# Feed-forward of one expert moved ahead of an attention, and the router with it

## The chip, the cores and the metric

One core of a Trainium2 chip runs the whole program in one launch. TensorE does the matrix products and transposes into PSUM, VectorE (DVE in the profile) and ScalarE (ACT) read PSUM and write SBUF, GpSimd (POOL) works in SBUF and issues some transfers, SyncE (SP) issues the others. Each engine runs its own instructions in order and waits on semaphores. The metric is the device time of one launch in microseconds.

## The reference

Four sequences (B = 4) of 512 tokens with 288 channels go through four transformer layers, with one conditioning vector for each sequence. All is float32. Each layer is

```
mod = silu(c) @ w_ada + b_ada                    # six rows of 288 per sequence
h   = ln(x) * (1 + scale_msa) + shift_msa
q, k, v = split(h @ w_qkv + b_qkv)               # 16 heads of 18
x  += gate_msa * (softmax(q k^T / sqrt(18)) v @ w_proj + b_proj)
h   = ln(x) * (1 + scale_mlp) + shift_mlp
x  += gate_mlp * ffn(h)
```

In layers 1 to 3 `ffn` is gelu(h W1 + b1) W2 + b2 with 1152 hidden channels. In layer 0 it is a mixture of four such experts: `h @ w_gate` gives four logits, the two highest get the softmax of the two as weights and the others zero, and the output is the weighted sum of all four experts, which are all computed for all tokens. The attention of layer 2 is written like the others.

## The kernel before

`plan` is a Python function that writes one list of steps, and `build` walks this list once for each engine: what a step does on an engine is queued there in the order of the list. So the order of `put` calls is the order on every engine, and the planner's work is to interleave generators. It keeps a planned TensorE time `pe[0]`, the sum of `PE_NS` over the steps put.

The index i = 4 * layer + sequence runs from 0 to 16. An iteration has two parts.

- Attention of i: `at_steps(i)` puts 16 `s2` steps (scores again, transposed, and exp on ScalarE, L1316) and `av` steps (L1721), and beside them `pre(i+1)`: the rows of the next sequence turned (`turnx`, L1644) and its q and k (`proj_qk`). `proj_v(i+1)` follows.
- Feed-forward of i - 1: `ffn_steps(i-1)` puts `fc1` steps (two weight tiles of 128 hidden channels by 256 tokens, 14 matmuls, L1817; gelu on ScalarE, L1353 and L1354; the low half `hid` on VectorE, L1590) and, two double tiles later, the `fc2` steps (L1832, with the bias at L1830). An expert has 18 tiles: two halves of the tokens by nine tiles. After each half `residual` scales two results by the gates (L1535, VectorE) and adds them to X (L1225, GpSimd). The loop `weave` runs these steps as the main line and lets others advance beside them whenever the planned time has gone on by their gap: `mid(i)` (output projection of i, residual, norm, turn of the rows for the feed-forward, in layer 0 the router; gap `MID_NS`, 3500 in the iterations 1 to 4) and `side`, the score stream of i + 1 (gap `S1_NS`, 5000).

The score stream `s1_steps` puts pairs of score matmuls (L1698), whose row maxima VectorE takes from PSUM (MX at L1470), and after every eight pairs a `rows` step (L1704, a turn of the maxima, with a transfer into QS). A sequence has 32 pairs. `at_steps` advances the stream one step at each `s2` and forces what a group of heads still lacks. The router `route(i)` is 28 narrow matmuls (`rt`, L1801), then small VectorE steps `rtk`, `rte`, an exp on ScalarE and `rtw`, which writes the gates CW.

Matrix products are done with weights split in two parts. A weight chunk is transferred into one of two buffers ST, cast by ScalarE (FH, L1346), its rest subtracted by GpSimd (FL, L1220) and its tail mended by VectorE (`fix`, L1365). Nine chunks make an expert; `prep_f` does one, and may write a place of FH only when the fc2 of the expert before has read it (`w_free`). The list `jobs` fixes the order in which weights are transferred, two jobs ahead; those of the feed-forward, three chunks in a job of seven transfers, are issued by SP, others by GpSimd. Background steps sit in `bg`; `finish_bg(1000)` at the end of an iteration puts all that is left.

In iteration 0 there is no feed-forward to run. The order is attention of sequence 0, `proj_v(1)`, and then `mid(0)` with the score stream of sequence 1 and the background advancing one step each at every step of `mid(0)`. Its end is the router of sequence 0. Iteration 1 is the attention of sequence 1, and then all four experts of sequence 0.

## Time and profile before

| | us |
|---|---|
| median of 3 runs | 2354.89 (2349.18 to 2356.09) |
| profiled execution | 2348.38 |
| its span | 2346.7 |
| TensorE busy | 2084.9 (89%) |
| VectorE busy | 1292.9 (55%) |
| ScalarE busy | 1159.1 (49%) |
| GpSimd busy | 485.3 (21%) |

Busy times are sums over the instructions of an engine within the span; matmuls are pipelined, so that a busy TensorE is not one at its peak. The granted clock of TensorE is given as a share of full speed, 2.4 GHz; 0.50 is its low level of 1.2 GHz. PE is TensorE, PEld its weight loads. Times within the span count from its start. In the profiled execution the attention of sequence 1 begins near 223 us, the feed-forward of sequence 0 near 275, and the attention of sequence 2 near 461.

### The profile page before, as it was taken

Reading aid. Unit: us, or ns where it says so; the run is one execution under the profiler, and the core shown is the slowest. Engines: PE = TensorE matmul, PEld = TensorE weight load, DVE = VectorE, ACT = ScalarE, POOL = GpSimd, SP = SyncE. Lnnn points to the kernel's source line nnn. Section 1 sums busy time; section 2 is a strip of 40 time slices with the busy share of each in tenths; the row PEclk is TensorE's granted clock in tenths of the full one; section 3 lists DMA queues with packets and bytes.
Section 4 is the critical chain, followed back from the end, with each engine's and each line's share of the span. In section 5 each row is a group of like instructions: output and inputs, shape, how many; then the busy total and the mean of one; then the engine's idle time right before and its main releaser. Section 6 shows DMA issues by size and latency. Waiting matters only on the chain.

```text
span 2346.7 us, 39460 instructions
## 1 busy us (share of the span) xinstructions
PE 2084.9 (89%) x15784; PEld 1536.6 (65%) x15784; DVE 1292.9 (55%) x2749; ACT 1159.1 (49%) x1797; POOL 485.3 (21%) x502
## 2 busy tenths in 40 slices
PE   6978999879989998999899999978988988899988
PEld 4443588738874886588466556877877637374748
DVE  3747355645664667465638482443424847674733
ACT  2353525554546365545635555534435273737363
POOL 3020033414440343044310100022210101100001
PEclk9685999989989998999998999997898989999999
DMA  4242422333234123423231412344253241323111
GB/s 147 61 132 47 115 67 69 78 90 97 68 97 112 52 86 64 119 68 89 72 98 14 125 7 62 42 92 103 44 109 58 72 90 37 83 44 88 31 14 24
DMA packets 204732, 173.99 MB, mean 74 GB/s; under 512 B 54822, under 2 KB 164678, under 8 KB 204550
## 3 DMA queue, kind: packets, MB, share of 16 engines
q1 hardware_dynamic: 197974, 158.76, 28.9%
q0 software_dynamic: 6576, 12.71, 1.9%
q8 instruction: 125, 2.05, 0.4%
q14 instruction: 57, 0.47, 0.1%
HBM read 125.57 MB, written 40.11 MB: 71 GB/s over the span
## 4 chain that ended last, share of the span: by engine, by line
PE 54%; DVE 21%; ACT 12%; issue 6%; POOL 3%; DMA 3%; SPq 2%; ACTq 0%; POOLq 0%; DVEq 0%
PE PSA L1817 13%; PE PSA L1832 9%; DVE MX L1470 8%; PE PSA L1721 6%; ACT PB L1316 4%; PE PSA L1668 4%; PE PSA L1611 4%; PE PSA L1711 4%; PE PSA L1698 4%; POOL FL L1220 2%; DVE HH L1590 2%; PE PSA L1634 2%; PE PSA L1741 1%; PE PSA L1680 1%; DVE FH L1365 1%
## 5 line engine op out<-in xcount | busy, mean ns | idle before, releaser
L1470 DVE TENSOR_REDUCE MX<-PSA 128x1 f32<-128x512 f32 x768 | 488.9, 683 | 317.5 <-PE PSA L1698 315.0
L1817 PE MATMUL PSA<-A,FH 128*128 128x256 f32 x2520 | 444.3, 291 | 26.1 <-DVE HH L1590 19.0
L1832 PE MATMUL PSA<-FH,HH 128*128 128x288 f32 x2016 | 449.5, 314 | 13.1 <-DVE HH L1590 13.0
L1353 ACT ACTIVATE HH<-PSA 128x512 fp32r<-128x512 f32 x252 | 150.3, 596 | 616.4 <-PE PSA L1817 609.2
L1316 ACT ACTIVATE PB<-PSA 128x1024 f32<-128x1024 f32 x384 | 370.7, 1027 | 103.3 <-PE PSA L1711 102.8
L1817 PEld LDWEIGHTS PSA<-A,FH 128*128 128x128 f32 x2520 | 363.8, 194 | 50.0 <-issue 20.1
L1832 PEld LDWEIGHTS PSA<-FH,HH 128*128 128x128 f32 x2016 | 331.0, 196 | 54.5 <-issue 36.6
L1832 PE MATMUL PSA<-FL,HH 128*128 128x288 f32 x1008 | 303.8, 301 | 0.0
L1220 POOL TENSOR_TENSOR FL<-ST,FH 128x544 fp32r<-128x544 f32 x171 | 240.2, 1418 | 233.9 <-ACT FH L1346 233.5
L1225 POOL TENSOR_TENSOR X<-X,TM 128x288 f32<-128x288 f32 x176 | 140.2, 811 | 681.0 <-DVE TM L1535 680.9
L1698 PE MATMUL PSA<-KS,QS 54*128 54x512 f32 x768 | 236.1, 528 | 41.4 <-DVE MX L1470 28.4
L1590 DVE TENSOR_TENSOR HH<-PSA,HH 128x512 fp32r<-128x512 f32 x252 | 172.7, 685 | 111.7 <-ACT PSA L1354 109.4
L1721 PE MATMUL PSA<-PB,VT 128*32 128x512 f32 x1536 | 227.7, 659 | 0.0
L1817 PE MATMUL PSA<-A,FL 128*128 128x256 f32 x1008 | 209.9, 290 | 14.8 <-POOL FL L1220 10.3
L1711 PE MATMUL PSA<-QS,KS 56*128 56x512 f32 x768 | 176.3, 508 | 50.7 <-ACT PB L1316 31.8
L1832 PEld LDWEIGHTS PSA<-FL,HH 128*128 128x128 f32 x1008 | 196.9, 195 | 0.0
L1711 PEld LDWEIGHTS PSA<-QS,KS 56*128 56x128 f32 x768 | 71.6, 202 | 168.7 <-ACT PB L1316 85.9
L1698 PEld LDWEIGHTS PSA<-KS,QS 54*128 54x128 f32 x768 | 98.6, 208 | 122.6 <-DVE MX L1470 65.0
L1817 PEld LDWEIGHTS PSA<-A,FL 128*128 128x128 f32 x1008 | 158.4, 194 | 23.1 <-POOL FL L1220 22.1
L1354 ACT ACTIVATE PSA<-PSA 128x512 f32<-128x512 f32 x252 | 149.3, 593 | 0.0
L1233 POOL COPY OT<-OT 128x256 f32<-128x256 f32 x16 | 6.5, 404 | 637.3 <-DVE OT L1489 507.0
L1346 ACT CAST FH<-ST 128x672 fp32r<-128x672 f32 x171 | 123.2, 748 | 29.1 <-DMA ST<-in_L_cond_w 13.9
(160 smaller groups left out, 2502.9 us busy)
## 6 DMA issues: line engine op xcount, KB each, us to landing
qkd<-HH SPq DMA_DIRECT2D x48, 504.0 KB
ST<-in_L_cond_w SPq DMA_DIRECT2D x51, 432.0 KB
ST<-in_L_cond_w SPq DMA_DIRECT2D x102, 192.0 KB
QS<-qkd SPq DMA_DIRECT2D x88, 144.0 KB
KS<-qkd SPq DMA_DIRECT2D x88, 144.0 KB
QS<-qkd SPq DMA_DIRECT2D x144, 72.0 KB
KS<-qkd SPq DMA_DIRECT2D x144, 72.0 KB
ST<-in_L_cond_w SPq DMA_DIRECT2D x153, 48.0 KB
```

The costliest lines, as they stand in the source:

```text
L1220: e.tensor_tensor(r(lo), ST[k % 2][:, s0:s0 + nl], hi[:, 0:nl], ALU.subtract).then_inc(s_wlo, 1)
L1225: e.tensor_tensor(X[:, b * QT + q, :], X[:, b * QT + q, :], TM[m % 2][:, :], ALU.add).then_inc(s_res, 1)
L1316: e.activation(pbf[st % 3][:, p * 1024:(p + 1) * 1024], PSA[:, bk * 512:(bk + 2) * 512], ACT.Exp, scale=SCALE).then_inc(free[bk], 1)
L1353: e.activation(r(HH[u][:, 0, :]), PS[bk][:, :], gelu)
L1354: e.activation(PS[bk][:, :], PS[bk][:, :], gelu).then_inc(s_gelu, 1)
L1470: e.reduce_max(MX[p // 2 % 2][:, col:col + 1], PS[bk][:, :], axis=AX.X).then_inc(free[bk], 1)
L1590: e.tensor_tensor(r(HH[u][:, 1, :]), PS[bk][:, :], HH[u][:, 0, :], ALU.subtract).then_inc(free[bk], 1)
L1698: e.matmul(PS[bk][:, :], r(QS[64 * x:64 * x + 54, p, q * 128:(q + 1) * 128]), r(KS[64 * x:64 * x + 54, p, :]), start=True, stop=True).then ...
L1711: m = e.matmul(PS[bk + x][:, :], r(KS[64 * x:64 * x + 56, 2 * g + p, kt * 128:(kt + 1) * 128]), r(QS[64 * x:64 * x + 56, 2 * g + p, :]), s ...
L1721: m = e.matmul(PS[bk][32 * hh:32 * hh + 32, :], VT[:, kt, h * V1:h * V1 + 32], PB[st % 3][:, hh, :], start=(kt == 0), stop=(kt == 3))
L1817: m = e.matmul(PS[bk][:, s_ * 256:(s_ + 1) * 256], r(w_), r(x_[:, half * 256:(half + 1) * 256]), start=(z == 0), stop=(z == 6))
L1832: m = e.matmul(PS[bk][:, 0:C], r(HH[u][:, c, tk]), r(w_), start=False, stop=(j == NCH - 1 and z == 2))
```

## The change

- In iteration 0 `mid(0)` runs with the score stream of sequence 1 and the background only until the rows for the feed-forward are turned (`rows_turned`). Since the test is made after a step has been taken, the router's matmuls `rt` are put as well.
- Then come `gates(0, 1)`, which was put in the attention of sequence 1, the switch to the PSUM banks `RING_B`, and `ffn_steps(0, (0,))`: expert 0 of sequence 0, with one step of `mid(0)` beside each of its steps and a step of the score stream per 2500 ns.
- `route(0)` stands before `stats_ahead(2)` in `mid(0)` and not behind it.
- Iteration 1 runs `ffn_steps(0, (1, 2, 3))`, with the score stream of sequence 2 at a gap of 4000 and not 5000.
- The weight job order brings the three jobs of expert 1 before the modulation weights of layer 1.

```diff
--- before.py
+++ after.py
@@ -28,6 +28,7 @@
 PE_NS = {"fc1": 1650, "fc2": 400, "proj": 930, "v": 930, "v2": 930, "qk": 1650, "turnx": 500, "turno": 500,
          "s1": 230, "s2": 450, "av": 230, "no": 500, "rows": 350, "qk2": 1650, "s1b": 1700, "s2b": 3000, "av2": 2500, "no2": 500, "rt": 3100}
 MID_NS = (3500, 800, 600)
+S1_0_NS = (0, 2500, 4000)
 S1_NS = (5000, 400, 3000)
 MID_AT = (8000, 14000)
 QK_LAND = 12000
@@ -135,12 +136,15 @@
     k_ = 3
     for i_ in range(NI + 1):
         L_, b_ = i_ // 4, i_ % 4
+        if i_ == 0:
+            jobs += [("f", k) for k in range(3, 6)]
+            k_ = 6
         if L_ < 3 and b_ == 1:
             jobs += [("ada", L_ + 1, j) for j in range(3)]
         if L_ < 3 and b_ == 2:
             jobs += [("q", L_ + 1), ("v", L_ + 1)]
         if 1 <= i_ <= 4 or (i_ and b_ == 0):
-            n_ = min(3 * NE if i_ <= 4 else 3, 4 * NE * 3 + 9 - k_)
+            n_ = min(9 if i_ == 1 else 3 * NE if i_ <= 4 else 3, 4 * NE * 3 + 9 - k_)
             jobs += [("f", k) for k in range(k_, k_ + n_)]
             k_ += n_
         if L_ < 3 and b_ == 3:
@@ -621,7 +625,7 @@
     back = background()
     n_fc, n_f1, n_f2 = [0], [0], [0]
 
-    def ffn_steps(i):
+    def ffn_steps(i, experts=None):
 
         L = i // 4
         a_n = (i + 1) % 2
@@ -629,7 +633,7 @@
         n_first = NCH * (i * NE if L == 0 else 16 + (L - 1))
         base = n_fc[0]
         tiles = [(e_, half, j, n_first + NCH * e_ + j)
-                 for e_ in range(NE if L == 0 else 1) for half in range(2) for j in range(NCH)]
+                 for e_ in experts or range(NE if L == 0 else 1) for half in range(2) for j in range(NCH)]
         nu = len(tiles) // 2
         acc, hid = [None] * 2, {}
 
@@ -704,7 +708,7 @@
                     next(side, None)
                     last[n] = pe[0] + gap
 
-    last_fc1, turned_early = [-1], set()
+    last_fc1, turned_early, rows_turned = [-1], set(), set()
 
     def pre(i):
         if i not in turned_early:
@@ -723,14 +727,16 @@
         for _ in range(W_MID):
             yield
         yield from turn_x(norm_of[i], (i + 1) % 2, L, 2, b)
+        rows_turned.add(i)
         if i + 2 < NI:
             if i == 0:
+                yield from route(0)
                 yield from stats_ahead(2)
             while i + 2 not in stats_of:
                 finish_bg(1)
             normed(i + 2, 0, stats_of[i + 2])
             yield
-        if L == 0:
+        if L == 0 and i:
             yield
             yield
             yield from route(i)
@@ -781,7 +787,7 @@
             for n, turned in enumerate(at2_steps(i) if L == 2 else at_steps(i)):
                 if L == 2 or n >= TURN_AT and not turned:
                     next(nxt, None)
-                if n == 3 and i:
+                if n == 3 and i > 1:
                     gates(i - 1, 1)
                 step_bg(2 if i == 0 else 1)
                 if i == 0 and not gb_ready[0] and (0, 0) in gr_ready:
@@ -816,9 +822,13 @@
             bg += [split(("q", L + 1), "q"), split(("v", L + 1), "v")]
         kind = 0 if i - 1 < 4 else 2 if (i + 1) // 4 == 2 else 1
         if i == 0:
-            weave(m, ((side, 0, 0), (back, 0, 0)))
+            weave(itertools.takewhile(lambda _: not rows_turned, m), ((side, S1_0_NS[0], 0), (back, 0, 0)))
+            gates(0, 1)
+            ring_of[0] = RING_B
+            weave(ffn_steps(0, (0,)), ((m, 0, 0), (side, S1_0_NS[1], 0)))
         if i:
-            weave(ffn_steps(i - 1), ((m, MID_NS[kind], MID_AT[i == 11] if L == 2 else 0), (side, S1_NS[kind], 0)))
+            weave(ffn_steps(i - 1, (1, 2, 3) if i == 1 else None), ((m, MID_NS[kind], MID_AT[i == 11] if L == 2 else 0),
+                                       (side, S1_0_NS[2] if i == 1 else S1_NS[kind], 0)))
         weave(m, ((side, S1_NS[kind], 0),))
         finish_bg(1000)
         if b == 3 and L < 3:
```

## Rows read from the trace of the kernel before

**Rows 1.** The page, part 1: busy us (share of the span) xinstructions.

```profile
PE 2084.9 (89%) x15784; PEld 1536.6 (65%) x15784; DVE 1292.9 (55%) x2749; ACT 1159.1 (49%) x1797; POOL 485.3 (21%) x502
```

**Rows 2.** Busy us (count) by engine in a stretch, clock, DMA share, GB/s.

```profile
192.50:223.00 30.50, 21.36 (x58) 12.43 (x57) 25.64 (x75) 3.72 (x9) 0.00 (x0) 0.50 0.01 4
...
223.00:275.00 52.00, 49.58 (x292) 21.85 (x292) 18.09 (x50) 38.12 (x47) 0.40 (x1) 0.93 0.44 95
...
345.00:383.00 38.00, 33.66 (x243) 30.63 (x242) 24.01 (x52) 19.38 (x35) 16.07 (x15) 1.00 0.28 79
...
461.00:478.00 17.00, 7.54 (x32) 2.73 (x34) 6.30 (x17) 7.77 (x9) 9.39 (x13) 0.63 0.42 71
...
1355.00:1385.00 30.00, 28.35 (x170) 21.20 (x169) 27.67 (x63) 15.06 (x30) 1.56 (x2) 1.00 0.15 8
```

**Rows 3.** Waits, 192 to 223: who waited for whom, us, times, longest.

```profile
PEld PSA L1698 <- DVE MX L1470: 11.9, 19, 1.7
...
PE PSA L1704 <- DVE MX L1470: 4.7, 2, 4.3
```

**Rows 4.** The chain of waits, 303 to 313: start, us, what.

```profile
303.69 1.67 PE PSA L1817 x14
...
311.53 1.59 PE PSA L1832 x12
```

**Rows 5.** Groups by line, 275 to 470: busy us, mean ns, idle before.

```profile
L1830 PE MATMUL PSA<-B,ON 128*128 128x288 f32 x16 | 5.4, 334 | 0.0
...
L1698 PE MATMUL PSA<-KS,QS 54*128 54x512 f32 x44 | 11.5, 518 | 0.0
...
L1590 DVE TENSOR_TENSOR HH<-PSA,HH 128x512 fp32r<-128x512 f32 x36 | 24.7, 687 | 13.2 <-ACT PSA L1354 12.7
...
L1535 DVE SCALAR_TENSOR_TENSOR TM<-PSA,CW,GB 128x288 f32<-128x288 f32 x16 | 7.5, 509 | 1.2 <-PE PSA L1832 1.2
...
L1365 DVE TENSOR_TENSOR FH<-ST,FH 33x128 fp32r<-33x128 f32 x36 | 17.5, 487 | 12.7 <-ACT FH L1346 11.9
...
L1377 DVE TENSOR_TENSOR B<-B2S,B 2x288 fp32r<-2x288 f32 x4 | 6.1, 1528 | 0.1
```

**Rows 6.** Instructions in order of time, 186 to 232: start, us.

```profile
187.72 0.29 DVE L1365 TENSOR_TENSOR FH<-ST,FH 33x128 fp32r<-33x128 f32 x1
...
191.76 0.68 DVE L1449 TENSOR_TENSOR A<-HF,A 32x512 fp32r<-32x512 f32 x1
...
205.87 0.99 PE L1801 MATMUL PSA<-WG,A 128*128 128x4 f32 x4
...
211.63 0.35 PE L1801 MATMUL PSA<-WG,A 96*128 96x4 f32 x1
...
222.96 1.69 PE L1711 MATMUL PSA<-QS,KS 56*128 56x512 f32 x4
...
223.80 3.91 ACT L1316 ACTIVATE PB<-PSA 128x1024 f32<-128x1024 f32 x4 [2.15 <-PE PSA L1711]
...
231.28 0.73 PE L1711 MATMUL PSA<-QS,KS 56*128 56x512 f32 x4
```

**Rows 7.** Line L1470 alone, 192.5 to 223: durations, first and last.

```profile
L1470 DVE TENSOR_REDUCE MX<-PSA x30: 657/682/692, 193.1 to 221.9; 128x1 f32<-128x512 f32 x30
```

**Rows 8.** Line L1365 alone, 275 to 470: ns min/median/max.

```profile
L1365 DVE TENSOR_TENSOR FH<-ST,FH x36: 282/290/1345, 330.8 to 464.7; 33x128 fp32r<-33x128 f32 x36
```

**Rows 9.** Order of time after the last fc2 of sequence 0.

```profile
462.58 2.06 ACT L1346 CAST FH<-ST 128x672 fp32r<-128x672 f32 x3 [4.23 <-DMA ST<-in_L_cond_w]
...
464.55 3.90 ACT L1316 ACTIVATE PB<-PSA 128x1024 f32<-128x1024 f32 x4
...
477.17 0.79 PE L1698 MATMUL PSA<-KS,QS 54*128 54x512 f32 x1 [5.98 <-DVE MX L1470]
```

**Rows 10.** Last residuals of experts 0 and 3, sequence 0.

```profile
344.49 0.93 DVE L1535 SCALAR_TENSOR_TENSOR TM<-PSA,CW,GB 128x288 f32<-128x288 f32 x2
...
460.30 0.94 DVE L1535 SCALAR_TENSOR_TENSOR TM<-PSA,CW,GB 128x288 f32<-128x288 f32 x2 [0.16 <-PE PSA L1832]
```

## The prediction

> **What bounds the kernel now.** I read the page first, then the busy time by stretch, then the waits and the instruction order inside the stretch that the change rewrites. TensorE is busy 89% of the span [rows 1], so in most places a microsecond is won only by removing TensorE work or TensorE idleness. The change removes no work; it can win only where TensorE idles or runs at its low clock. In time order the part concerned is:
>
> - 155 to 223: `mid(0)` with the scores of sequence 1. From 192.5 to 223 VectorE is busy 25.6 of 30.5 us, while the granted clock is 0.50, the 1.2 GHz level [rows 2]. The waits name the row maxima, MX at L1470, as what the score matmuls waited for, 11.9 us over 19 waits, and the last turn of the maxima waited 4.3 us for one [rows 3]. VectorE sets the pace here; TensorE has room.
> - 223 to 275: attention of sequence 1, TensorE 49.6 of 52 us.
> - 275 to 461: the four experts of sequence 0 beside `mid(1)`. In a plain expert (345 to 383) TensorE is busy 33.7 of 38 us at clock 1.00, VectorE 24.0: TensorE sets the pace [rows 2].
> - 461 to 478: a start of attention in which TensorE does 7.5 us in 17 [rows 2].
>
> So the change moves one expert from a TensorE-paced stretch into a VectorE-paced one.
>
> **What one expert weighs.** Nine double tiles of 14 fc1 matmuls, 1.67 us, and 12 fc2 matmuls, 1.59 us [rows 4], are 29.3 us; four bias matmuls at 0.334 add 1.3 [rows 5]: 30.6 us of TensorE. On VectorE it brings nine `hid` at 0.687 (6.2), four residuals at 0.509 (2.0), nine `fix` at 0.487 for the next expert's weights (4.4) and the bias split, its longest part 1.5 and in all about 3 by my estimate from that row: 15.6 us [rows 5]. ScalarE's GELUs and casts and GpSimd's subtractions have room: ScalarE has 3.7 us and GpSimd none in the 30.5 us [rows 2].
>
> **The first stretch.** Up to the turn of the rows the order is as before; the last piece of it is the DVE op at 191.76, and the last weight chunk of expert 0 has its tail fixed at 187.72 [rows 6], so nothing of expert 0 is late. From 192.5 on I build the new stretch:
>
> - The router comes first. It took from 205.87 to 211.98, 6.1 us at the low clock [rows 6]. Nothing denser stands around it now than before: 6.1. VectorE has nothing to do meanwhile.
> - The expert, 30.6.
> - Scores. 30 maxima are left after 192.5 [rows 7], 15 pairs. The side is allowed one step per 2500 ns of planned time over 9 x (1650 + 4 x 400) = 29250 ns; with steps of 1650 and 800 that comes out as nine, of which eight are pairs and one is the turn of the maxima. The 44 matmuls of L1698 between 275 and 470 are busy 11.5 us, 0.26 each [rows 5]: eight pairs are 4.2, and with the turn some 4.4.
> - The expert starts at the low clock. At 223 dense work began at that level too: four matmuls at L1711 took 1.69 us at 222.96 and 0.73 at 231.28 [rows 6], 8 us later. I take some 6 us of work done at half pace: 3 more.
> - Stalls. A plain expert leaves 38.0 - 33.7 = 4.3 us of idleness [rows 2], for its chain of GELU, hid and fc2; here, with more on VectorE, 5.
>
> Sum 6.1 + 30.6 + 4.4 + 3 + 5 = 49.1 us in the place of 30.5: **+18.6**. Bounds: below, without ramp and with half the stalls, 43.6 (+13). Above, VectorE decides. Its work from 192.5 is 16 maxima (10.9), route and statistics about 9, the expert's 15.6, the rest 1.5: 37 us; at the density of the old stretch, 25.6 of 30.5 or 84%, it takes 44, and with the 6 us of the router in which it has nothing, 50. So the two engines come out level, and the bound above comes from the fixes, next.
>
> **The fixes.** The `fix` at L1365 takes 290 ns in the median and up to 1345 [rows 8], in a stretch where GpSimd writes FL right beside it. GpSimd has such work after 192.5 only in the new kernel. If each of nine fixes took 1.345, they would be 12.1 us and not 4.4, all ahead of maxima in VectorE's queue; VectorE's 37 become 45, the stretch 45 / 0.84 + 6 = 59 us, +29. I keep the mean row, since 36 fixes at 0.487 already hold the long ones; +29 is the end above. The Trainium skill, "SBUF — State Buffer", section "Who interferes with whom", says that a VectorE instruction with two SBUF inputs is locked out while a GpSimd instruction reads SBUF; these operations are such a pair, and the long fixes here agree with it.
>
> **The boundary to the attention of sequence 1.** The expert leaves three casts of the next expert's weights in front of the first exps. At the same kind of boundary, after 460.5, ScalarE waited 4.23 us for a weight transfer, cast until 464.6, and the first exp began at 464.55 [rows 9], 4.0 us after the last fc2; before, at 223, it came about 1 us after. +3. Queued behind are exps, so the score-probability matmuls wait. On SP three loads of seven weight issues now stand ahead of the transfers of the turned maxima; these are needed only in the attention. Seven score pairs have slid into this attention, 3.5 us of TensorE, which is busy 95% there: +3. It now starts at the full clock: the slow beginning between 223 and 231 is spared, -3. Bounds 0 to +8, value **+3**.
>
> **The stretch of three experts.** It loses 30.6 us of TensorE and one of four sets of chain and weight-change stalls. A plain period is (460.30 - 344.49) / 3 = 38.6 us [rows 10], of which about 2 us of scores and 2.5 us of `mid(1)` stay: -34. What could also be late: the plan hands one piece of `mid(1)` per 3500 ns; four experts fit about 31 of its 34 pieces, three only some 24. The whole router of sequence 1 then comes after the last fc2. It runs about 3 us on TensorE, work that exists in either kernel, and its small VectorE chain, some 4 us, holds up ScalarE's exp and the exps behind it. But there TensorE stood until 477.17 for maxima anyway [rows 9], so of 5 us I count 1. Value **-33**, bounds -36 to -28.
>
> **Sum.** 18.6 + 3 - 33 = -11.4 us. The profiled execution took 2348.4 us around a span of 2346.7; the median of three is 2354.9, 6.5 above it. Taken off the median: 2343.5. Since the three runs spread over 7 us, I say 2344.
>
> **Rivals.**
> 1. *VectorE decides the first stretch* (chance 0.20). For it: 84% busy before and nine more hid. Against it: a later stretch, 1355 to 1385, with one expert, scores and the other sequence's `mid`, runs VectorE at 27.7 and TensorE at 28.4 of 30 us at clock 1.00 [rows 2]. With stalls of 12 for 5: net -4, 2351; no measurable change.
> 2. *Every fix is a long one* (0.08), by GpSimd's reads beside it. Against it: the mean row. Net 29 + 3 - 33 = -1: 2354. The lock is the one that the page named with the fixes states.
> 3. *The weights land late, slower* (0.12). The third load of expert 1 can be issued only when the first load's last chunk is split, and this waits for fc2 tiles in the second half of expert 0. If it lands more than 13 us after the last fc2 (2 of casts behind it, against 1 us before: 14 in place of 3, and the gain is gone), ScalarE's in-order queue holds every exp of the attention; at 461 a jam of this kind cost TensorE 9.5 of 17 us [rows 2]. For it: that jam, and more issues on SP. Against: there the GpSimd queue and a waiting residual were part of it, and SP is free. A landing at 21 us costs 22 in place of 3: net +8, 2362.
> 4. *The clock stays low* (0.07). If waits for maxima keep TensorE at 1.2 GHz, as between 192.5 and 223, expert 0 costs 30 us more in place of 3: net +16, 2371. Against: clock 1.00 with VectorE busier still at 1355 [rows 2]. The Trainium skill ("TensorE: Matmul & The Clock Gate", "What's actually happening") says the low level is the default and activity releases it; the trace agrees in both stretches.
> 5. *It does not do what it says* (0.03): expert 0 waits for its weights or the gate row. 187.72 speaks against it. 2355.
>
> **Numbers.** Forecast 0.50; no change means within 0.3%, 7 us, about what a measurement can tell. The forecast case itself is faster by that in some 8 of 10, rival 1 in 3 of 10: faster 0.48. Same 0.32, slower 0.20, from rivals 3, 4 and part of 1 and 2. Range 2332 (both low bounds, -22) to 2362; the likeliest case's own is 2334 to 2354.
>
> **What would show it.** Right: nine fc1 groups between about 198 and 235 with granted clock 1.00 from about 206; the first exp of the attention at 240 to 246 instead of 223.8; seven pairs of maxima in the first half of that attention; only two weight changes in the next FFN stretch, which ends 8 to 14 us earlier than 460.5; `rt` of sequence 1 right after its last fc2. Wrong: clock 0.5 past 215 (rival 4), `fix` near 1.3 us on the mean (2), ScalarE waiting over 10 us on a weight transfer near 245 (3), or an attention after 460 whose exps start more than 5 us later relative to the last fc2 and push 477.17 along with them.

## The result, and the profile after

| | before | after |
|---|---|---|
| median (lowest to highest), us | 2352.41 (2349.18 to 2356.09, 4 runs) | 2327.69 (2324.43 to 2334.02, 4 runs) |
| ratio to before, 95% interval | | 0.9904 (0.9874 to 0.9934) |
| span of the profiled execution, us | 2346.7 | 2332.3 |

The kernel became 1% faster, twice what was forecast, and its time lies below the range. The page, part 1, and then the busy time by stretch (TensorE, its weight loads, VectorE, ScalarE, GpSimd, then granted clock, DMA share, GB/s) of the kernel after; they answer to [rows 1] and [rows 2]. The stretches are the router, expert 0 with scores, the attention of sequence 1, the three experts, and 17 us after the last fc2 of sequence 0.

```profile
PE 2071.9 (89%) x15784; PEld 1533.1 (66%) x15784; DVE 1297.3 (56%) x2749; ACT 1164.2 (50%) x1801; POOL 484.8 (21%) x502
```

```profile
197.50:203.60 6.10, 6.04 (x29) 6.04 (x29) 0.00 (x1) 0.00 (x0) 0.00 (x0) 0.50 0.70 88
203.60:248.60 45.00, 38.97 (x256) 34.93 (x257) 34.05 (x82) 21.35 (x37) 12.39 (x13) 0.91 0.19 28
248.60:302.10 53.50, 47.52 (x280) 19.68 (x280) 32.50 (x67) 40.33 (x48) 7.00 (x8) 0.90 0.30 102
305.90:448.40 142.50, 133.84 (x941) 119.64 (x940) 76.87 (x151) 59.15 (x104) 47.73 (x44) 0.94 0.26 75
448.40:465.40 17.00, 9.71 (x52) 5.84 (x51) 10.87 (x38) 7.71 (x11) 8.38 (x12) 0.65 0.48 86
```

The expert stretch of before by the same view, for the comparison that decides:

```profile
274.80:460.60 185.80, 173.46 (x1208) 155.90 (x1206) 101.42 (x196) 77.18 (x134) 64.14 (x58) 0.93 0.26 74
```

The profiles do not locate the whole gain. From the end of the turn of the rows to the end of the span it is 2154.3 us before and 2134.8 after, 19.5 less, and 2151.1 and 2133.5, 17.6 less, in a second pair of profiles (again_before, again_after), where the medians differ by 24.7 and 29.2. The ledger below accounts for the 17 to 20; where the rest sits no profile shows.

**One table of marks for all runs.** What lies before the turn of the rows differs by 9 us between executions whose order there is the same (the turn ends between 188.6 and 197.5), so I count from that turn. Its end is the end of the VectorE step that stands at 191.76 in [rows 6]: 192.4. Marks: A, first L1711 of the attention of sequence 1 (L1721 after); V2, next values product; F, first fc1 of the experts in iteration 1; R, end of their last fc2; V3, the values product after it; V6, the values product at the end of iteration 4. All in us, from one profile each; V2 to F is 3.7 to 3.8 everywhere.

| kernel | turn-A | A-V2 | F-R | R-V3 | turn-V3 | V3-V6 | timed ratio |
|---|---|---|---|---|---|---|---|
| before | 30.5 | 48.1 | 185.8 | 67.4 | 335.5 | 663.2 | 1 |
| after | 51.1 | 53.4 | 142.5 | 62.4 | 313.3 | 668.2 | 0.9904 |
| again_before | 30.5 | 48.2 | 185.7 | 67.5 | 335.7 | 662.6 | one run |
| again_after | 51.1 | 53.7 | 139.9 | 64.1 | 312.6 | 665.9 | 0.9878 |
| late_route | 30.5 | 47.8 | 179.2 | 70.6 | 332.0 | 666.4 | 0.9963 |
| before_gap_4000 | 30.5 | 48.2 | 188.5 | 56.3 | 327.4 | 671.3 | 0.9986 |
| before_both | 30.5 | 48.1 | 183.4 | 58.2 | 324.0 | 667.3 | 0.9967 |
| early_route | 51.1 | 54.1 | 157.9 | 59.9 | 326.7 | 668.8 | 0.996 |
| gap_5000 | 51.1 | 53.7 | 140.2 | 86.8 | 335.6 | 666.1 | one run |
| gap_3000 | 51.1 | 54.2 | 153.0 | 59.4 | 321.5 | 670.3 | 0.9959 |
| q_sp_gap_5000 | 51.1 | 53.8 | 140.1 | 77.9 | 326.7 | 666.0 | 0.997 |
| scores_dense | 54.0 | 57.2 | 144.1 | 65.5 | 324.6 | 667.6 | one run |
| b2_first | 47.7 | 53.5 | 147.9 | 65.1 | 318.0 | 671.4 | 0.9934 |
| rt_later | 45.8 | 52.8 | 141.3 | 62.4 | 306.1 | 667.6 | 0.9883 |
| rt_b2 | 47.2 | 53.6 | 142.5 | 68.1 | 315.2 | 660.3 | 0.9857 |
| rt_b2_q_sp | 47.2 | 54.0 | 138.5 | 62.9 | 306.4 | 657.4 | 0.984 |
| combined | 47.3 | 54.1 | 138.5 | 67.9 | 311.5 | 653.4 | 0.984 |
| all_four | 47.2 | 53.7 | 142.6 | 64.4 | 311.8 | 652.4 | 0.9812 |

The first two columns repeat within 0.8 us between kernels with the same order there. F-R does not always: 142.5 and 139.9 in two executions of the changed kernel. A difference under 4 us there is no finding. The two profiles say what differed:

```profile
302.90:442.80 139.90, 131.20 (x942) 116.60 (x940) 76.85 (x151) 59.15 (x104) 47.71 (x44) 0.96 0.28 77
```

That is again_after, against the fourth line above: the same matmuls and, to 0.1, the same 8.7 us of idleness, with 2.6 us less of TensorE busy at a granted clock of 0.96 and not 0.94. So when F-R or R-V3 of two kernels are compared, busy time, idle time and clock have to be taken apart; I do so where a reading rests on it.

After against before: +20.6, +5.3, -43.3, -5.0 up to V3, in sum -22.2 by the marks, and +5.0 given back up to V6 (+3.3 in the second pair).

**The first stretch.** Order of time around 200 us on TensorE, after (start us, duration us, what; the idle time before it in brackets):

```profile
197.56 1.02 PE L1811 MATMUL PSA<-WG,A 128*128 128x4 f32 x4 [3.41 <-DVE A L1459]
...
203.56 1.20 PE L1827 MATMUL PSA<-A,FH 128*128 128x256 f32 x4
...
209.35 0.28 PE L1827 MATMUL PSA<-A,FH 98*128 98x256 f32 x1
...
241.57 0.54 PE L1842 MATMUL PSA<-FH,HH 128*128 128x288 f32 x2 [4.02 <-DVE HH L1600]
```

The router takes its 6.1 us; from 203.56 on work is dense, and its groups of four fc1 matmuls go from 1.20 to 0.71 us (granted clock 0.50 from 203 to 206, 0.69 to 209, 1.00 to 212). One long wait is left, 4.02 us for a `hid`. Here is what VectorE did in it, and beside it GpSimd:

```profile
233.74 1.35 DVE L1384 CAST B<-B2S 2x288 fp32r<-2x288 f32 x1
235.12 1.65 DVE L1387 TENSOR_TENSOR B<-B2S,B 2x288 fp32r<-2x288 f32 x1
236.81 1.35 DVE L1390 CAST B<-B2S 1x288 fp32r<-1x288 f32 x1
238.09 1.27 DVE L1480 TENSOR_REDUCE MX<-PSA 128x1 f32<-128x512 f32 x2
239.38 1.41 DVE L1375 TENSOR_TENSOR FH<-ST,FH 33x128 fp32r<-33x128 f32 x1
240.82 0.69 DVE L1600 TENSOR_TENSOR HH<-PSA,HH 128x512 fp32r<-128x512 f32 x1
```

```profile
235.11 5.53 POOL L1230 TENSOR_TENSOR FL<-ST,FH 128x544 fp32r<-128x544 f32 x4 [0.19 <-ACT FH L1356]
```

The bias split, 4.35 us in three operations, stands ahead of the `hid`, and so do the two maxima and a `fix` of 1.41 us. Line L1384 by itself shows that it need not be so long: four times, 298 ns at least, 299 in the median, 1349 at most.

```profile
L1384 DVE CAST B<-B2S x4: 298/299/1349, 233.7 to 439.2; 2x288 fp32r<-2x288 f32 x4
```

The two maxima, which read PSUM, keep their 0.64 us each beside the same GpSimd work.

**The attention of sequence 1** starts as said, with a late exp. ScalarE in order of time; it answers to [rows 9]:

```profile
248.44 2.06 ACT L1356 CAST FH<-ST 128x672 fp32r<-128x672 f32 x3 [4.62 <-DMA ST<-in_L_cond_w]
250.52 1.28 ACT L1326 ACT_TABLE_LOAD   x1
251.81 3.91 ACT L1326 ACTIVATE PB<-PSA 128x1024 f32<-128x1024 f32 x4
```

Of the delay, 1.28 us is a load of ScalarE's function table (ACT_TABLE_LOAD), since GELUs now stand ahead of these exps; the kernel has 35 such loads and had 31. The attention also starts at the low clock level again: its four matmuls of L1721 at 252.89 take 1.71 us, like those of L1711 at 222.96 in [rows 6].

### The profile page after: what moved, and what is told of

Read it like the earlier page. It is cut to its first block, busy times and chain, and to the rows that moved or that the text cites. A ratio compares the mean times of both kernels' runs of the same rounds, so it can differ in the third digit from the quotient of the medians.

```text
span 2332.3 us, 39462 instructions
## 1 busy us (share of the span) xinstructions
PE 2071.9 (89%) x15784; PEld 1533.1 (66%) x15784; DVE 1297.3 (56%) x2749; ACT 1164.2 (50%) x1801; POOL 484.8 (21%) x502
## 4 chain that ended last, share of the span: by engine, by line
PE 54%; DVE 20%; ACT 12%; issue 5%; DMA 4%; POOL 3%; SPq 2%; ACTq 0%; POOLq 0%; DVEq 0%
PE PSA L1827 13%; PE PSA L1842 10%; DVE MX L1480 8%; PE PSA L1731 5%; PE PSA L1621 4%; ACT PB L1326 4%; PE PSA L1721 4%; PE PSA L1678 4%; PE PSA L1708 3%; POOL FL L1230 2%; PE PSA L1644 2%; DVE HH L1600 2%; DVE FH L1375 2%; PE PSA L1751 1%; PE PSA L1690 1%
## 5 line engine op out<-in xcount | busy, mean ns | idle before, releaser
L1480 DVE TENSOR_REDUCE MX<-PSA 128x1 f32<-128x512 f32 x768 | 489.1, 682 | 324.0 <-PE PSA L1708 321.6
L1708 PE MATMUL PSA<-KS,QS 54*128 54x512 f32 x768 | 225.3, 516 | 31.9 <-DVE MX L1480 20.0
L1827 PE MATMUL PSA<-A,FL 128*128 128x256 f32 x1008 | 210.5, 291 | 15.5 <-POOL FL L1230 9.6
L1721 PE MATMUL PSA<-QS,KS 56*128 56x512 f32 x768 | 174.4, 505 | 55.3 <-ACT PB L1326 36.1
L1721 PEld LDWEIGHTS PSA<-QS,KS 56*128 56x128 f32 x768 | 70.8, 201 | 172.0 <-ACT PB L1326 90.2
L1708 PEld LDWEIGHTS PSA<-KS,QS 54*128 54x128 f32 x768 | 93.8, 204 | 106.3 <-DVE MX L1480 47.7
L1375 DVE TENSOR_TENSOR FH<-ST,FH 33x128 fp32r<-33x128 f32 x171 | 104.9, 623 | 53.9 <-ACT FH L1356 49.6
```

Of the source, the lines that this page charges most:

```text
L1375: e.tensor_tensor(r(hi[64:R2 - 1, f0:f0 + nf]), ST[k % 2][64:R2 - 1, s0 + f0:s0 + f0 + nf], hi[64:R2 - 1, f0:f0 + nf], ALU.subtract).then_ ...
L1480: e.reduce_max(MX[p // 2 % 2][:, col:col + 1], PS[bk][:, :], axis=AX.X).then_inc(free[bk], 1)
L1708: e.matmul(PS[bk][:, :], r(QS[64 * x:64 * x + 54, p, q * 128:(q + 1) * 128]), r(KS[64 * x:64 * x + 54, p, :]), start=True, stop=True).then ...
L1721: m = e.matmul(PS[bk + x][:, :], r(KS[64 * x:64 * x + 56, 2 * g + p, kt * 128:(kt + 1) * 128]), r(QS[64 * x:64 * x + 56, 2 * g + p, :]), s ...
L1827: m = e.matmul(PS[bk][:, s_ * 256:(s_ + 1) * 256], r(w_), r(x_[:, half * 256:(half + 1) * 256]), start=(z == 0), stop=(z == 6))
```

## The experiments

In the line numbers of the changed kernel ten are added to those of before, in its variants up to 21; in variants of the kernel before three or fewer.

**1 and 2. Both kernels again.** No edit.

> The kernel before once more, for a second trace. Theory: turn to end of the attention of sequence 2 again 335 us within 2; the last fc2 of sequence 0 to the end of that attention 67 us; the turn anywhere from 190 to 198. Rival: the jam after the last fc2 is a matter of this one execution; then 67 becomes 55 and the stretch is some 12 us shorter.

> The changed kernel once more, for a second trace and a tighter ratio. Theory: the whole gain lies between the turn of sequence 0's rows and the end of the attention of sequence 2 (before 192.4 to 528.0, 335.5 us; after 313.3), and what the first trace shows ahead of it (+5.1 us) is not of the change. Expected: that stretch again 311 to 315 us, the start of it anywhere from 190 to 198, the time 22 us below before (ratio 0.990 to 0.992). Rival, that the +5 ahead is caused by the changed order of the weight transfers: the turn again at 197 to 198.

Before 2348.13 us in one run, after 2325.74, ratio 0.9878 (0.9859 to 0.9897). The marks repeat: the gain and its places are not an accident of one execution. The turn of the changed kernel's rows ends at 194.3 here and not at 197.5, so that the late turn of the first profile is not of the change.

**3. late_route.** The kernel before, with the router of sequence 1 after the last fc2, where the changed kernel has it.

```diff
+            while i == 1 and ffn_done[0] < 0:
+                yield
             yield from route(i)
```

> The kernel before, and in iteration 1 the router of sequence 1 waits until the last fc2 of sequence 0 is put. It tests where the 9 us come from by which the stretch of three experts fell short of my sum. Theory A (the router's place): beside the experts the router costs TensorE 3 to 4 us and its chain more, while after them it is hidden by GpSimd's jam (weight issues for layer 1, then the waiting residual); then this alone gives -4 to -9 us: first fc1 to last fc2 from 185.8 to 177 to 182, last fc2 to the end of the attention 67.4 within 2. Rival B: nothing to gain there, the router's chain is added after the experts as fast as it leaves them: 0 within 3 us in all.

2345.97 us, 0.9963 (0.9938 to 0.9987). The experts take 6.6 us less, the stretch after them 3.2 more. Where the 6.6 sit is to be read in the chain of waits of the kernel before, 411 to 450:

```profile
415.95 1.59 PE PSA L1832 x12
...
428.16 3.02 PE PSA L1801 x28
431.18 0.58 PE PSA L1698
431.76 3.14 PE PSA L1832 x12
434.90 1.67 PE PSA L1817 x14
```

The 28 narrow matmuls cost 3.02 us, and the twelve fc2 matmuls behind them 3.14 in place of 1.59. In the stretch of before from 421 to 440 the granted clock was 0.91, from 345 to 421 it was 1.00; in the changed kernel it is 1.00 from 345 to 448. So the router costs TensorE its own 3.0 us and, after it, 1.5 us at the low clock level. Much of the rest stands near the end of the last expert, the kernel before first, then late_route:

```profile
455.05 0.73 PE L1832 MATMUL PSA<-FH,HH 128*128 128x288 f32 x2 [2.30 <-DVE HH L1590]
```

```profile
447.37 0.54 PE L1835 MATMUL PSA<-FH,HH 128*128 128x288 f32 x2 [0.96 <-DVE HH L1593]
```

In the kernel before two operations of the router's gates (L1554 and L1557, 1.36 us from 452.99 on) stand ahead of that `hid` on VectorE; TensorE waits 1.3 us longer and then works from 455 to 459 at a granted clock of 0.57, where late_route has 1.00 from 430 to the last fc2. Over the whole of F-R TensorE is busy 6.0 us less in late_route and idle 0.5 less: 3.0 are the router's own matmuls, the other 3.0 the same matmuls at a higher granted clock.

**4. early_route.** The changed kernel with the gap of `mid(1)` at 2300 and not 3500, so that the router comes while the three experts run.

```diff
-            weave(ffn_steps(i - 1, ...), ((m, MID_NS[kind], ...
+            weave(ffn_steps(i - 1, ...), ((m, 2300 if i == 1 else MID_NS[kind], ...
```

> The changed kernel, with mid(1) in iteration 1 at a gap of 2300 and not 3500, so that its router runs beside the three experts as before. Theory A: the router comes back onto the experts' stretch, first fc1 to last fc2 from 142.5 to 147 to 151, the rest unchanged or a jam of 5 to 7 us more in the attention: +4 to +9 us in all. Rival B: 0 within 3.

2343.27 us, 0.996 (0.9937 to 0.9983): more than half of the gain is gone. F-R is 15 to 18 longer, more than the theory's 4 to 9, R-V3 2.5 to 4 shorter. Of the 15 to 18, 4.3 are idleness of TensorE (13.0 for 8.7) and 11 to 14 are busy time (144.9 us for 133.8 and 131.2; the router's own matmuls are some 3 of it, the granted clock is 0.88 for 0.94 and 0.96). All of `mid(1)` moved up with the router, so that this run tells what dense company costs the experts, not what the router costs alone. The late part of its experts:

```profile
423.00:462.00 39.00, 34.11 (x191) 31.42 (x190) 21.59 (x42) 12.75 (x21) 11.66 (x10) 0.72 0.15 41
```

**5. gap_5000.** The changed kernel with the old gap for the scores of sequence 2.

```diff
-S1_0_NS = (0, 2500, 4000)
+S1_0_NS = (0, 2500, 5000)
```

> The changed kernel, with the score stream beside the three experts at the gap of 5000 as before and not 4000. Theory (scores further ahead are part of the gain): about four pairs fewer get done beside the experts; first fc1 to last fc2 1 to 2 us shorter, last fc2 to the end of the attention of sequence 2 from 62.4 or 64.1 to 67 to 71, +2 to +6 in all. Rival (the gap does not matter): both within 1.5 us of after.

2351.9 us in one run: the whole gain is gone, far more than I had given this edit. The experts are no shorter than in again_after (140.2 for 139.9), but what follows takes 86.8 for 62.4. Thirty score matmuls stand beside the three experts and not 40, so that 36 are left. TensorE by line from R to V3, and the waits in the 40 us after R (us in total, times, longest):

```profile
L1721 PE MATMUL PSA<-QS,KS 56*128 56x512 f32 x64 | 14.6, 523 | 13.9 <-DMA QS<-M 8.3 <-ACT PB L1326 5.3
L1708 PE MATMUL PSA<-KS,QS 54*128 54x512 f32 x36 | 9.1, 471 | 10.9 <-DVE MX L1480 8.9 <-DVE HH L1474 2.0
```

```profile
POOL ST L1220 <- issue: 13.3, 2, 11.7
DVE BN L1410 <- POOL X L1235: 11.8, 1, 11.8
...
PE PSA L1708 <- DVE MX L1480: 8.9, 1, 8.9
```

The same view of the changed kernel has 26 score matmuls and no wait for maxima:

```profile
L1708 PE MATMUL PSA<-KS,QS 54*128 54x512 f32 x26 | 5.7, 444 | 0.0
```

A late stream pays three times: the scores that are left, the turned maxima that the attention waits for (8.3 us for the transfer into QS), and a jam of VectorE's statistics behind GpSimd, which is issuing weight transfers. In all TensorE stands 30.2 us between R and V3 where it stood 10.5, and is busy 4.6 more.

**6. rt_later.** The changed kernel, `route(0)` three steps later.

```diff
+                for _ in range(3):
+                    yield
                 yield from route(0)
```

> The changed kernel, with three steps of the expert between the turn of the rows and the router of sequence 0, so that the router's narrow matmuls come beside fc1 and not ahead of it. Theory (the low clock is a price of the order): the router ran 6.1 us at the 1.2 GHz level with nothing beside it; behind two fc1 groups it runs at the high level in 3 to 4 us and VectorE is not idle in it: turn to first attention matmul from 51.1 to 47 to 49 us, the rest within 1. Rival: the low level lasts just as long from whatever comes first; 51 within 1.

2324.18 us, 0.9883 (0.984 to 0.9925), not to be told from the changed kernel by time alone. The first stretch is 5.3 us shorter, in a column that otherwise repeats to 0.1, and 45.8 us is below the 47 to 49 expected: the router now stands behind three double tiles, at the full level, from 197.07 to 200.12, 3.05 us for 6.1.

```profile
197.07 0.51 PE L1813 MATMUL PSA<-WG,A 128*128 128x4 f32 x4
...
200.01 0.25 PE L1813 MATMUL PSA<-WG,A 96*128 96x4 f32 x1
```

**7. b2_first.** The changed kernel, the bias split put ahead of the first cast, with two steps in front of it for its transfer (the one step that followed the split goes, so that each expert's preparation has one step more).

```diff
+        if n_ % NCH == 0:
+            yield
+            yield
+            put("b2", n_ // NCH, b2_free.get(n_ // NCH % 2))
         if x == 0:
             yield from arrive(("f", k))
...
-        if n_ % NCH == 0:
-            put("b2", n_ // NCH, b2_free.get(n_ // NCH % 2))
-            yield
```

> The changed kernel, with the three VectorE operations that split an expert's second bias put ahead of the first weight chunk's subtraction on GpSimd, not behind it. Theory P (port): GpSimd's subtraction locks out VectorE operations with SBUF inputs; in the trace of after these three took 1.35, 1.65 and 1.35 us beside FL, the hid behind them was late and TensorE stood 4.0 us, then ran at the low clock. Freed, they take about 0.4 each: turn to first attention matmul from 51.1 to 46 to 49 us, first fc1 to last fc2 from 142.5 or 139.9 to 130 to 137, and as this happens at 19 experts, 10 to 25 us less in all. Rival V (VectorE is merely full there, and what does not block is replaced by the next in the queue): within 1 us in each stretch and 3 in all.

2335.25 us, 0.9934 (0.9911 to 0.9957). The first stretch is 3.4 shorter, as the 4.02 us wait let hope, but the experts take 5 to 8 more where they were to take 3 to 12 less. Of the 5 to 8, 3.4 are idleness of TensorE (12.1 us for 8.7: waits of fc1 for the parts of its weights 8.0 for 6.2, waits for a `hid` 2.5 for 1.1) and the other 2 to 4.6 the same matmuls at a granted clock of 0.93, for 0.94 and 0.96. So the added step delays the weights by 1.8 us, a part of the loss and not all of it.

**8. scores_dense.** The changed kernel, a score step at each step of expert 0.

```diff
-S1_0_NS = (0, 2500, 4000)
+S1_0_NS = (0, 0, 4000)
```

> The changed kernel, with no gap for the scores of sequence 1 beside expert 0 (0 and not 2500): all 15 pairs run beside the expert, none slides into the attention. Theory (TensorE paces up to eight pairs, VectorE beyond): seven more pairs are 9.6 us of VectorE on 34.0 busy of 51.1, over its limit: turn to first attention matmul 56 to 60, the attention of sequence 1 from 53.5 to 49 to 51; +2 to +5 in all. Rival (VectorE has room): 54 to 55 and 49 to 50, 0 in all.

2343.42 us in one run; first stretch +2.9, as the rival had it (54.0), but attention 1 +3.8 where both had expected it shorter. Counted from the turn, the last three casts of weights start at 59.8 us and not at 50.9, 8.9 later where the expert itself is 2.9 later, and ScalarE waits 8.24 us for them where it waited 4.62. In SyncE's queue four transfers of turned maxima, issued from 242.12 to 244.77, now stand directly ahead of the last weight load; in the changed kernel none does. They take 2.7 of the 6 us by which the casts slip beyond the expert; the rest is not traced.

```profile
253.79 2.06 ACT L1356 CAST FH<-ST 128x672 fp32r<-128x672 f32 x3 [8.24 <-DMA ST<-in_L_cond_w]
...
257.16 3.91 ACT L1326 ACTIVATE PB<-PSA 128x1024 f32<-128x1024 f32 x4
```

**9. before_gap_4000.** The kernel before with the new gap in iteration 1.

```diff
-            weave(ffn_steps(i - 1), (..., (side, S1_NS[kind], 0)))
+            weave(ffn_steps(i - 1), (..., (side, 4000 if i == 1 else S1_NS[kind], 0)))
```

> The kernel before with one number changed: in iteration 1 the score stream of sequence 2 has the gap 4000 and not 5000, so some five more of its steps fall beside the four experts. Theory (the move of the expert carries the gain, and 4000 only keeps the stream from falling behind when one expert is gone): in the kernel before 28 score matmuls follow the last fc2, with the gap 4000 some 18; the experts take 2 to 3 us more, the stretch from the last fc2 to the next values product 3 to 5 less, from turn to V3 334 to 336 in place of 335.6, ratio 0.998 to 1.001. Rival (the gap is the gain): the stretch after the last fc2 falls by 10 or more, from turn to V3 at most 325, ratio 0.995 or less.

2348.5 us, 0.9986 (0.9968 to 1.0004). Neither theory: up to V3 it wins 8.1 us (R-V3 -11.1, F-R +2.7; 12 score matmuls left for 28), and by V6 it has given back 8.1, 5.8 of it in iteration 2 (226.8 for 221.0). In iteration 2 TensorE is busy 4.6 us more (206.0 for 201.4, at a granted clock of 0.95 and not 0.97) and idle 1.2 more; why the clock is lower there is open.

**10. gap_3000.** The changed kernel with the gap 3000.

```diff
-S1_0_NS = (0, 2500, 4000)
+S1_0_NS = (0, 2500, 3000)
```

> The changed kernel with the gap 3000 in place of 4000 in iteration 1: some five to seven more steps of the score stream beside the three experts. Theory (at 5000 the stream fell behind, at 4000 it has enough): experts +2 to +4 us, the stretch after the last fc2 -2 to -4, from turn to V3 312 to 315. Rival 1 (VectorE is the bound beside the router): experts +8 or more, as the early router did, from turn to V3 above 320. Rival 2 (the stretch after the last fc2 is still short of maxima at 4000): it falls by 8 or more, from turn to V3 at most 307.

2340.73 us, 0.9959 (0.9941 to 0.9977). Rival 1's numbers, not its cause: the experts are 10.5 to 13 longer, but TensorE idles only 0.8 us more than in the changed kernel.

```profile
302.20:455.20 153.00, 143.54 (x980) 126.03 (x979) 90.49 (x169) 61.14 (x106) 48.76 (x46) 0.91 0.28 74
```

Ten more score matmuls (50 for 40) are 2.6 us at the 0.26 of [rows 5]. The edit also does something that its one number does not tell: as the scores add to the planned time, `mid(1)` advances faster, and the router of sequence 1 comes at 445.24, ahead of the last fc2 and not behind it. Its 28 matmuls are 3.1 us there; what is left goes with the granted clock, 0.91 for 0.94 and 0.96. So 4000 lies between two steep sides, at 3000 the experts pay, at 5000 the attention, but at 3000 the router's place and the gap were not told apart.

**11. q_sp_gap_5000.** As gap_5000, layer 1's q weights issued by SP.

```diff
-        return jobs[k][0] == "f" or k < SP_JOBS
+        return jobs[k][0] == "f" or k < SP_JOBS or jobs[k] == ("q", 1)
```

(the same condition at the two places that issue, and at the wait of the cast)

> The changed kernel with the gap 5000, and the seven or so transfers of layer 1's q weights issued by SP and not by GpSimd. With the gap 5000 alone the stretch from the last fc2 to the next values product took 86.8 us in place of 62.4, with GpSimd waiting to issue weight transfers in front of its adds and its transfer of the turned maxima. Theory (GpSimd's queue makes a late stream dear): the stretch falls to 60 to 68 us. Rival (36 score matmuls and their maxima after the last fc2 are dear by themselves, through VectorE's and TensorE's order): it stays at 78 or above.

2341.28 us, 0.997 (0.9948 to 0.9992); R-V3 77.9 for 86.8 and 62.4, which is the rival's number. GpSimd's queue is 8.9 of the 24.4 us: TensorE's wait of 8.9 us for a maximum is gone, at the same busy time. The late stream itself is the other 15.5; the waits for the transfer into QS stay (8.1 for 8.3).

**12. combined.** Three edits on the changed kernel: experiment 6; the bias split ahead without steps of its own (the next expert's bias is fetched two chunks early, the first one as before); the routers of sequences 2 and 3 after their last fc2.

```diff
-        if n_ % NCH == 0:
-            put("b2in", k, n_ // NCH)
+        if n_ == 0 or n_ % NCH == 7:
+            put("b2in", ...)
+        if n_ and n_ % NCH == 0:
+            put("b2", n_ // NCH, b2_free.get(n_ // NCH % 2))
...
+            while i in (2, 3) and ffn_done[0] < i - 1:
+                yield
```

> The changed kernel with three edits meant to win: route(0) three steps later (so that it stands beside fc1), the bias split ahead of GpSimd's subtraction without further steps (its transfer is issued two chunks earlier), and the routers of sequences 2 and 3 after their last fc2 too, as that of sequence 1 is by itself. Theory, from the ledgers: -5.3 us (router) and -3 (bias split) in the first stretch, -3 to -4 in each of the two FFN stretches net of what their routers cost later: from turn to V3 301 to 305, the rest after V3 6 to 8 us shorter, ratio 0.980 to 0.983. Rival: a router behind the last fc2 costs there what it saved (no gain after V3) and the earlier bias transfer delays GpSimd's adds: ratio 0.986 to 0.989.

2309.91 us, 0.984 (0.981 to 0.987). The ratio lies between theory and rival. Up to V3 it is worse than said (311.5, R-V3 67.9), from V3 to V6 better: 653.4 for 668.2. The first stretch, 47.3, is 1.5 longer than with the later router alone (rt_later, 45.8), so the early bias split saved nothing there. The bias operations of the experts of sequence 3 (by line: busy us, mean ns, idle before), the changed kernel first, then this one:

```profile
L1387 DVE TENSOR_TENSOR B<-B2S,B 2x288 fp32r<-2x288 f32 x4 | 6.1, 1531 | 0.1
L1390 DVE CAST B<-B2S 1x288 fp32r<-1x288 f32 x4 | 3.3, 824 | 0.1
L1384 DVE CAST B<-B2S 2x288 fp32r<-2x288 f32 x4 | 2.3, 585 | 0.1
```

```profile
L1395 DVE CAST B<-B2S 2x288 fp32r<-2x288 f32 x4 | 2.9, 731 | 0.0
L1398 DVE TENSOR_TENSOR B<-B2S,B 2x288 fp32r<-2x288 f32 x4 | 1.8, 448 | 0.1
L1401 DVE CAST B<-B2S 1x288 fp32r<-1x288 f32 x4 | 1.2, 298 | 0.1
```

11.7 us of VectorE became 5.9, and over all 19 experts 51.2 became 27.2.

**13. before_both.** The kernel before with both companions of the move, the edits of experiments 3 and 9, and without the move.

> The kernel before with both companions of the move and without the move: the router of sequence 1 put after the last fc2, and the gap 4000 for the scores of sequence 2. If they add as measured alone: experts 185.8 - 6.6 + 2.7 = 182, from the last fc2 to V3 67.4 + 3.2 - 11.1 = 60, from turn to V3 some 324, ratio 0.995 to 0.998; the difference to the changed kernel, 313.3, then is the expert's move alone, some -11 us. Rival (the companions are all of it): from turn to V3 at most 317. Rival (they cancel when together, both crowd the stretch after the last fc2): at least 331.

2343.67 us, 0.9967 (0.9948 to 0.9986). From turn to V3 324.0: up to there the two edits add (335.5 - 3.5 - 8.1 = 323.9). Up to V6 they don't: each alone has given its gain back by then (-0.3 and 0.0 by the marks), together they keep 7.4. 52 score matmuls stand beside the four experts and 14 after them; the changed kernel has 40 beside three. By stretch:

```profile
275.90:459.30 183.40, 170.79 (x1193) 152.18 (x1191) 101.24 (x193) 76.94 (x133) 64.00 (x59) 0.94 0.26 74
459.30:476.30 17.00, 11.13 (x61) 6.43 (x64) 8.98 (x33) 6.25 (x9) 7.54 (x12) 0.61 0.48 84
```

**14. rt_b2.** The combined version without the late routers of sequences 2 and 3.

> As the combined version, but the routers of sequences 2 and 3 stand beside the experts again. The combined version's iterations 2, 3 and 4 took 218.3, 219.4 and 215.7 us in place of 222.9, 224.9 and 220.4; the fourth has no router. Theory (the bias split ahead of GpSimd's subtraction carries it, 4 to 5 us in each stretch): the three stay within 1 us of the combined version's, ratio 0.983 to 0.986. Rival (the late routers carry half): the first two are 2 us or more longer, the third unchanged.

2317.02 us, 0.9857 (0.9835 to 0.9879). Iterations 2, 3 and 4: 220.8, 222.9 and 216.6, where the combined version has 218.3, 219.4 and 215.7 and the changed kernel 222.9, 224.9 and 220.4. The rival's numbers: the bias split brings 2, 2 and 4, the late routers another 2.5 and 3.5. With the second profile of each pair (again_after 222.9, 223.5, 219.5; rt_b2_q_sp 219.3, 222.8, 215.4; all_four 218.1, 219.2, 215.1) the bias split brings 2.1 to 3.6, 0.6 to 2.1 and 2.9 to 5.0, the late routers 1.0 to 2.7 and 3.4 to 3.7. The timed ratios of rt_b2 and combined do not tell the two apart.

**15. rt_b2_q_sp.** The same with SP for layer 1's q weights.

> As the run with the later router(0) and the early bias split, and the transfers of layer 1's q weights issued by SP. Theory (GpSimd's issue waits hold adds and the transfer of the maxima after the last fc2): from the last fc2 to V3 some 60 us, 6 to 8 less than the same without the edit, ratio 0.980 to 0.983. Rival (with the gap 4000 the maxima are ahead and nobody waits for GpSimd): within 2 us of the same without the edit.

2311.73 us, 0.984 (0.9809 to 0.9871). R-V3 62.9 for 68.1, 5.2 less where the theory had 6 to 8, and not by its mechanism. R-V3 of rt_b2 first, then of this run:

```profile
439.10:507.20 68.10, 56.35 (x311) 26.65 (x312) 42.59 (x96) 42.19 (x53) 15.05 (x19) 0.82 0.39 91
```

```profile
433.50:496.40 62.90, 51.84 (x312) 24.22 (x312) 40.59 (x96) 41.94 (x53) 9.03 (x10) 0.89 0.44 99
```

TensorE idles 11.1 us for 11.7; the other 4.5 are the same matmuls at a higher granted clock. That SP's issues gave this is not shown.

**16. all_four.** The combined version with SP for the q weights.

> The combined version with the transfers of layer 1's q weights issued by SP. If the edits add: from turn to V3 some 303 us (311.5 less the 8.8 that SP's issues gave beside the early bias split), iterations 2 to 4 together 653 to 656, ratio 0.978 to 0.982. Rival: SP's issues pay back part later, as iteration 3 of the run without late routers shows (222.8 against 222.9, no gain): ratio 0.982 to 0.985, no better than the combined version.

2310.7 us, 0.9812 (0.9787 to 0.9837), the lowest ratio of the study, and its interval lies under those of both runs of the changed kernel. From turn to V3 it is no better than combined (311.8, where 303 was expected; F-R 142.6 for 138.5 eats what R-V3 gains, and both differences are busy time of the same matmuls, at 0.93 for 0.96 and 0.87 for 0.82), so that the fourth edit is not shown to add to the other three.

## Why the prediction was wrong

It said -11.4 us and the time fell by 24.7, of which the profiles locate 17 to 20. Point by point:

- *First stretch, +18.6*: +20.6. Router 6.1 as said; TensorE busy 39.0 us from 203.6 to 248.6 against 38.0 in my terms (30.6, 4.4 and the ramp of 3), idle 6.0 against 5. The eight pairs came out as counted (16 score matmuls), and so did the seven left for the attention (14 of its 22; the other 8 are sequence 2's). I had blamed the fixes for what can go wrong; the one long wait came from the bias split, which I had entered at 3 us and which took 4.35 in one piece. (The low end of my range was 13.1 + 0 - 36 = -22.9, which gives its 2332; the -22 beside it is a slip.)
- *Boundary, +3*: +5.3. The first exp stands 54.3 us after the turn, 31.4 before; ScalarE's wait for weights was 4.62, near the 4.23 of [rows 9], from which I had taken the term. I had no term for the table load of 1.28 us, and the 3 us that I took off for a start at the full clock were not spared: the granted clock is 0.90 over this attention, 0.93 before.
- *Three experts with the attention behind, -33, bounds -36 to -28*: -48.3 and, in the second pair of profiles, -49.2. **This is the step that failed.** The difference of the changed kernel to before_both splits it. The move itself is -40.9 in F-R and +4.2 in R-V3, -36.7: just outside the lower bound, about as reckoned. The other -11.6 are the two things that come with it. Together they give -2.4 in F-R, with 12 more score matmuls in it, and -9.2 in R-V3 (before_both against before), where TensorE idles 7.6 us for 15.4. The split holds with the gap at 4000. With the gap at 5000 and the late router the move adds 3.6 us up to V3 (gap_5000 335.6, late_route 332.0) and the gap then takes 22.3: the two work together, and which of them the gain is put down to depends on the order in which they are added.
- The sentence that missed the first was "of 5 us I count 1". I priced the late router where it lands and not where it leaves. It leaves 6.6 us beside the experts (late_route). It does land as I feared: the router holds ScalarE from 450.2 to 458.6, and the first exp comes 12.3 us after the last fc2, before 4.0:

```profile
448.91 1.28 ACT L1347 ACT_TABLE_LOAD   x1
458.60 0.22 ACT L1347 ACTIVATE GE<-GL 128x16 f32<-128x16 f32 x1 [8.41 <-DVE GL L1577]
458.72 2.04 ACT L1356 CAST FH<-ST 128x672 fp32r<-128x672 f32 x3
460.67 3.90 ACT L1326 ACTIVATE PB<-PSA 128x1024 f32<-128x1024 f32 x4
```

Only the last 3.4 us of that wait are the VectorE chain, which I had put at some 4; before it the router's matmuls waited for a row maximum until 451.23 and ran until 455.1:

```profile
451.23 0.58 PE L1811 MATMUL PSA<-WG,A 128*128 128x4 f32 x4 [2.15 <-DVE MX L1480]
...
455.17 0.17 DVE L1551 COPY GL<-PSA 128x16 f32<-128x16 f32 x1 [2.30 <-PE PSA L1811]
```

- The second has no sentence. The gap 4000 stood in my text only as "about 2 us of scores" that stay; what it takes away after the last fc2, the 5.98 us wait for maxima of [rows 9], got no term. In R-V3 it is worth 24.4 us in the changed kernel (gap_5000) and 11.1 in the kernel before; up to V3 that is 22.3 and 8.1. The clearest sign was in my own rows: TensorE did 7.5 of 17 us there [rows 2], and I took this wait as cover for the router, not as something that the change could remove. Without the smaller gap the move gains nothing up to V3: 335.6 from turn to V3 against 335.5.
- *Up to V3* the sum is -22.2, the move -10.7 of it (313.3 for 324.0), near the -11.4 that I put down for everything. Up to V6 it is -17.2 and, in the second pair, -19.8. The companions alone (before_both) save 11.5 up to V3, 7.4 up to V6 and 7.8 in the timed runs.

**The rivals.** 1, VectorE decides: no; it was busy 34.05 of 45 us, less than TensorE, and held TensorE 4.6 us. 2, long fixes: one took 4.756 us, beside an add and three subtractions of GpSimd, but at 249.2, after the last fc2, where no matmul of the expert waited for it. The rule I gave of the Trainium skill ("SBUF — State Buffer", "Who interferes with whom") also says that a cast can take both ports in its fast mode; the trace agrees, 1.35 us for L1384 beside the subtraction and 0.298 alone, and this is what put the bias split on the path (b2_first, with the split ahead of the subtraction, has the first stretch 3.4 us shorter). 3, late weights: 4.62 us, no jam; 8.24 when the scores were pressed (scores_dense). 4, low clock: 1.00 from 209 to 242. 5, no.

Of the signs that I named, the granted clock rose from 1.2 to 2.4 GHz at about 208, 10 us after the turn, with the work dense from 203.56, and I had said 206, 14 us after a turn at 192.4; the stretch of experts ended 12.2 us earlier in the span (448.4 for 460.6), or 17.3 counted from the turn. One sign of being wrong came true by half: the exps start 8.3 us later relative to the last fc2 than before, more than the 5 that I had named, yet R-V3 is 5 us shorter.

## What to carry to other kernels

When a step moves from one place to another, price the place that it leaves as carefully as the one it joins: a narrow-matmul router inside dense work cost 6.6 us there, twice its own duration. A constant that comes along with a reordering can hold the whole gain, so put it by itself into the kernel before and take it out of the kernel after. Read a long wait in the stretch behind the change as a term that the change may remove or double, not as cover. And before a wait is named as the cause of a difference, take TensorE's idle time, busy time and granted clock of the stretch apart: several differences here that looked like waits were the same matmuls at another clock.

## What the runs showed of the hardware

- Behind the 28 matmuls of the router, 3.02 us of back-to-back work on TensorE, twelve fc2 matmuls took 3.14 us for 1.59, the pace of the 1.2 GHz level, though TensorE had idled only 1 us in the 8 before. This does not always follow: in the 7 us behind the same 28 matmuls the granted clock stayed at 1.00 in rt_later (200.3 to 207.3) and in before_gap_4000 (438.5 to 445.5). The router itself ran in 3.05 us behind dense fc1 and in 6.1 at the low level.
- VectorE's cast of two partitions by 288 from SBUF took 0.298 us alone and 1.349 beside a GpSimd subtraction that had begun before it; where the subtraction began 0.22 us after it (547.5 in the changed kernel) it took 0.297. Its reduction from PSUM took 0.64 in both places. Putting the bias split before the subtraction halved its time on VectorE, 11.7 to 5.9 us per four experts.
- A `fix` of 0.29 us at 249.2 in the changed kernel took 4.756: GpSimd's add had begun just before it, and three subtractions, each begun after it, also ran before it ended.
- The stretch F-R of the changed kernel differed by 2.6 us between two executions, at a granted clock of 0.94 and 0.96, and everything before the turn by up to 9, with the order unchanged; the stretch from the turn to the first attention matmul repeated to 0.1 in five executions of the old order and six of the new.
